# A four-layer graph network on one core: layer 0's preparation cut into pieces beside the second edge sort, and three of TensorE's turns in layer 3 placed behind a group's second pair of slots

## The reference

```
edge_index = jnp.stack([src, dst])
h = jnp.maximum(_layernorm(x, axis=-1), 0.0)
x = x + _L0_gnn_ref(h, edge_index, W, att_src, att_dst, bias)
...            # layers 1, 2 and 3 in the same way
```

```
h = (x @ W.T).reshape(N, H, C)                    # 4 heads of 64 channels
a_s = jnp.einsum('nhc,hc->nh', h, att_src)
a_d = jnp.einsum('nhc,hc->nh', h, att_dst)
e = jax.nn.leaky_relu(a_s[src] + a_d[dst], 0.2)
m = jax.ops.segment_max(e, dst, num_segments=N)
p = jnp.exp(e - m[dst])
alpha = p / (segment_sum(p, dst)[dst] + 1e-16)
out = segment_sum(alpha[:, :, None] * h[src], dst)
return elu(out + bias) + x
```

## Time and profile before

| | |
|---|---|
| median of 3 runs | 4839.82 us (4831.98 to 4845.45) |
| the profiled execution | 4839.27 us |
| its span | 4837.5 us |
| mean granted TensorE clock | 0.702 |
| busy: PE, DVE, ACT, POOL | 3143.0, 3130.4, 2247.6, 2855.6 us |

### The profile page before, as it was taken

The page is one execution under the profiler, slowest core; times in us unless marked ns, Lnnn a source line. Parts: engine busy times, 40 slices in busy tenths (PEclk is TensorE's granted clock), DMA queues, the critical chain, the costliest instruction groups (busy, mean ns, idle before and its releaser), DMA issues. The chain is left out here.

```text
span 4837.5 us, 75613 instructions
## 1 busy us (share of the span) xinstructions
PE 3143.0 (65%) x14588; PEld 2278.2 (47%) x14668; DVE 3130.4 (65%) x10392; ACT 2247.6 (46%) x8908; POOL 2855.6 (59%) x2739
## 2 busy tenths in 40 slices
PE   1588875777614666654777774466652677778776
PEld 0366664665512444443554453244431456566565
DVE  5887775666544555564777765476665477777776
ACT  0355554555422443344666664243334255555555
POOL 0377776777706777733777761777770265555532
PEclk9855556555556777676767767677776788888889
DMA  1000000000014444423454541444450476666641
GB/s 51 1 2 2 2 2 2 2 2 2 2 47 132 133 132 126 126 53 97 138 145 138 146 113 62 125 132 132 121 115 4 162 204 182 180 177 175 178 110 62
DMA packets 235835, 449.09 MB, mean 93 GB/s; under 512 B 80264, under 2 KB 132390, under 8 KB 235110
## 3 DMA queue, kind: packets, MB, share of 16 engines
q0 software_dynamic: 130816, 317.16, 25.1%
q1 hardware_dynamic: 104752, 128.89, 8.2%
HBM read 416.04 MB, written 29.80 MB: 92 GB/s over the span
## 5 line engine op out<-in xcount | busy, mean ns | idle before, releaser
L1239 POOL DMA_INDIRECT rows.4<-feats,by_dst_other.1 x464 | 506.2, 1091 | 537.8 <-issue 321.2
L1239 POOL DMA_INDIRECT rows.2<-feats,by_dst_other.1 x464 | 495.4, 1068 | 281.3 <-POOLq L976 140.2
L1239 POOL DMA_INDIRECT rows.1<-feats,by_dst_other.1 x464 | 493.4, 1063 | 280.7 <-POOLq L976 139.6
L1239 POOL DMA_INDIRECT rows.3<-feats,by_src_other.1 x448 | 476.4, 1063 | 256.9 <-issue 129.2
L658 POOL DMA_INDIRECT by_dst_records<-r_rec.1,r_idx.1 x448 | 443.8, 991 | 160.4 <-issue 127.7
L658 POOL DMA_INDIRECT by_src_records<-r_rec.2,r_idx.2 x416 | 413.9, 995 | 144.1 <-issue 113.4
L1455 ACT ACTIVATE rows.4<-rows.4,xres.1 128x65 f32<-128x65 f32 x1856 | 447.9, 335 | 0.9
L1455 ACT ACTIVATE rows.2<-rows.2,e_prob.2 128x33 f32<-128x33 f32 x1856 | 397.9, 314 | 0.0
L1370 PE MATMUL m_p.4<-rows.4,xres.1 128*128 128x264 f32 x1044 | 337.3, 451 | 30.9 <-issue 18.5
L1351 PE MATMUL m_p.3<-rows.3,m_oh.3 128*128 128x260 f32 x896 | 314.5, 505 | 13.9 <-DVE rows.3 L1604 13.0
L1622 DVE TENSOR_TENSOR acc.4<-acc.4,m_p.4 128x528 f32 x261 | 183.5, 703 | 198.3 <-PE m_p.4 L1387 155.9
(11 more groups left out here) (763 smaller groups left out, 8262.7 us busy)
## 6 DMA issues: line engine op xcount, KB each, us to landing
e_line.1<-by_dst_own_row SPq DMA_DIRECT2D x29, 512.0 KB, 5.0
e_line.2<-by_dst_own_row SPq DMA_DIRECT2D x29, 512.0 KB, 4.4
e_line.4<-by_dst_own_row SPq DMA_DIRECT2D x58, 256.0 KB, 5.2
e_line.3<-by_src_own_row SPq DMA_DIRECT2D x28, 512.0 KB, 5.0
xres.1<-by_dst_masks SPq DMA_DIRECT2D x232, 48.0 KB
e_mask.2<-by_dst_masks SPq DMA_DIRECT2D x29, 320.0 KB
rows.1<-feats,by_dst_other.1 POOLq DMA_INDIRECT x464, 2.8
rows.2<-feats,by_dst_other.1 POOLq DMA_INDIRECT x464, 3.9
```

The lines of the kernel that those rows point to most:

```text
L1239: pool.indirect_dma_start(out=rows[:, s % RING, :], out_offset=None, in_=feats, in_offset=bass.IndirectOffsetOnAxis(ap=g.other[:, s:s + 1] ...
```

## The change

Two things change.

**Layer 0's preparation.** A class `Front` holds what `read_sorted` does for `by_dst` and what layer 0's two blocks of norm and product do, as pieces with a batch number n. The second `place_edges` (that of `by_src`) gets it: ACT, PE and DVE run all 104 batches written out, without a loop, and do piece n behind batch n. POOL keeps its loop. The reading of the sorted edges has the batches 0 to 21, the norm 22 to 33, and tile t of the product begins at batch 34 + 8t // 3, with its steps in the five batches from there on; the last one ends in batch 102. The two PSUM banks of the finished histograms serve all of it (`by_lo` for turned tiles, `by_other` for products), one bank each where the product had two. SP issues the loads, the stores of masks and joins and the stores of the 25 tiles in the same block. Behind the second sort stands `read_sorted` for `by_src` alone, and then layer 0's `stream_edges`.

**Layer 3's turns.** With `LATE`, the turns 0, 1 and 2 of layer 3 stand behind the group's second pair and its closing; `turn_back` stays between the pairs. The order of DVE, ACT, POOL and SP in layer 3 is the same as before.

```diff
+        front = Front(nc, sig, sb, first, C, T, [hist[g].sums for g in graphs])
+        place_edges(nc, sig, sb, ps, second, C, B, T, None, front)
+    read_sorted(nc, sig, sb, ps, second, C)
-        place_edges(nc, sig, sb, ps, second, C, B, T, None)
-    for g in graphs:
-        read_sorted(nc, sig, sb, ps, g, C)
...
+class Front:
+    def tile_at(self, t):
+        return 34 + t * 8 // 3
...
+    def scalar(self, act, n):
...
+        if n in range(22, 27):
+            i = n - 22
+            act.wait_ge(S["steps"].sem, self.nmean_at(i))
...
+            for j in range(5):
+                t = 5 * i + j
+                ins = act.activation(self.sq[:, j, :], xres[:, t, :], ACT.Square, bias=self.nmean[:, t:t + 1], accum_out=self.ss[:, t:t + 1])
...
+            if n == self.tile_at(t) + 2:
+                act.wait_ge(S["tile_turned"].sem, S["tile_turned"].at(t + 1))
...
+                act.activation(self.hT[:, par, :, :], self.by_lo[:, 0:2 * P].rearrange("p (k q) -> p k q", k=2), ACT.Copy).then_inc(S["copied"].sem, 1)
+            if n == self.tile_at(t):
...
+                act.activation(self.hst[:, par, :], xres[:, t, :], ACT.Relu, bias=self.shift[:, t:t + 1],
+                               scale=self.rstd[:, t:t + 1]).then_inc(S["staged"].sem, 1)
+    def tensor(self, pe, n):
...
+            if n == self.tile_at(t) + 3:
+                pe.wait_ge(S["copied"].sem, S["copied"].at(t + 1))
+                if t >= 1:
+                    pe.wait_ge(S["evacuated"].sem, S["evacuated"].at(t))
...
+                for k in range(2):
+                    ins = pe.matmul(self.by_other[:, 0:CH + 8], self.hT[:, par, k, :], self.wall[:, k, :], start=k == 0, stop=k == 1)
+                ins.then_inc(S["product"].sem, 1)
+            if n == self.tile_at(t) + 1:
+                pe.wait_ge(S["staged"].sem, S["staged"].at(t + 1))
...
+                    ins = pe.transpose(self.by_lo[:, k * P:(k + 1) * P], self.hst[:, par, k * P:(k + 1) * P], ident[:, :])
+                ins.then_inc(S["tile_turned"].sem, 1)
+    def vector(self, dve, n):
...
+            if n == self.tile_at(t) + 4:
+                dve.wait_ge(S["product"].sem, S["product"].at(t + 1))
...
+                dve.tensor_copy(C["own0"][:, t, :], self.by_other[:, CH + 4:CH + 8]).then_inc(S["evacuated"].sem, 1)
...
@@ place_edges
+            if front is not None and eng_front is not None:
+                for i in range(trips):
+                    for quarter in range(Q):
+                        for part in parts:
+                            part(i * Q + quarter, quarter, i)
+                        eng_front(eng, i * Q + quarter)
+                return
...
@@ gat_layer_in
+    if n > 0:
+        norm_and_product(nc, sig, sb, ps, A, K, n, convs, heads0, wide, row0, own, feats)
...
@@ stream_edges
+    LATE = (NC == 2, NC == 2, NC == 2, False)
...
                         for k, turn in enumerate(turns):
-                            if AT[k] == i - 1:
+                            if AT[k] == i - 1 and not LATE[k]:
                                 turn(c + 1)
                     if PAIRS:
                         opening(s0 + 4 * i + 2, group + 1)
...
+                    if c + 1 < NCH:
+                        for k, turn in enumerate(turns):
+                            if AT[k] == i - 1 and LATE[k]:
+                                turn(c + 1)
```

More of the change, by code:

```diff
@@ L514, in place_edges, with _, turns @@
         trips = g.cols // (Q * B)
-        def turns(eng, parts, beside):
+        if front is not None:
+            front.place(c2)
+            @block.sync
+            def _(sp):
+                front.sync(sp)
+        def turns(eng, parts, beside, eng_front=None):
             def batches(i, ps):
@@ L566, in _ @@
             table(0, 0, 0)
-            turns(act, [ahead(diagonals, 2), ahead(table, 1), records], [])
+            turns(act, [ahead(diagonals, 2), ahead(table, 1), records], [], front and front.scalar)
         @block.tensor
@@ L607, in _ @@
             count(0, 0, 0)
-            turns(pe, [ahead(spread, 1), look, ahead(count, 1)], [lambda n, quarter, i: other.count(pe, n, quarter % 2)])
+            turns(pe, [ahead(spread, 1), look, ahead(count, 1)], [lambda n, quarter, i: other.count(pe, n, quarter % 2)], front and front.tensor)
         @block.vector
@@ L644, in _ @@
             onehots(0, 0, 0)
-            turns(dve, [before_in_column, ahead(onehots, 1), place], [lambda n, quarter, i: other.onehots(dve, n, quarter % 2)])
+            turns(dve, [before_in_column, ahead(onehots, 1), place], [lambda n, quarter, i: other.onehots(dve, n, quarter % 2)], front and front.vector)
         @block.gpsimd
@@ L669, in place_edges @@
         gate.base += Q * trips
+        if front is not None:
+            front.close()
 def read_sorted(nc, sig, sb, ps, g, C):
@@ L807, in gat_layer_in, with norm_and_product @@
     ROW = FROM + HS
-    own = sb("own_scores", [P, T, HS], F32, lc)
-    feats = nc.dram_tensor(f"feats{n}", [NT, ROW], F32, kind="Internal").ap()
+    own = K["own0"] if n == 0 else sb("own_scores", [P, T, HS], F32, lc)
+    feats = K["feats0"] if n == 0 else nc.dram_tensor(f"feats{n}", [NT, ROW], F32, kind="Internal").ap()
+    if n > 0:
+        norm_and_product(nc, sig, sb, ps, A, K, n, convs, heads0, wide, row0, own, feats)
+    with ExitStack() as c:
+        acc = sb("acc", [P, T, NC * max(wide) + (HS if n == 1 else 0)], F32, c)
+        stream_edges(nc, sig, sb, ps, K, n, g, convs, heads0, row0, own, feats, acc)
+        if n == 3:
+            finish_last(nc, sig, sb, ps, A, K, convs, acc, out)
+        elif n == 1:
+            finish_global(nc, sig, sb, ps, K, convs, acc)
+        else:
+            finish_layer(nc, sig, sb, ps, A, K, n, convs, acc)
+def norm_and_product(nc, sig, sb, ps, A, K, n, convs, heads0, wide, row0, own, feats):
+    N, T, NT, LAST = K["N"], K["T"], K["NT"], K["LAST"]
+    xres, ident = K["xres"], K["ident"]
+    NC = len(convs)
+    FEAT = NC * CH
+    HS = sum(c[1] for c in convs)
+    WALL = FEAT + 2 * HS
+    FROM = sum(wide)
+    ROW = FROM + HS
     steps, roots = sig("norm_steps"), sig("norm_roots")
@@ L1082, in gat_layer_in @@
             he.base += T + 2
-            hx.base += T if n in (0, 3) else 0
+            hx.base += T if n == 3 else 0
             for j in range(2):
                 st[j].base += 16 * (T // 2 + (1 - j) * (T % 2))
-    with ExitStack() as c:
-        acc = sb("acc", [P, T, NC * max(wide) + (HS if n == 1 else 0)], F32, c)
-        stream_edges(nc, sig, sb, ps, K, n, g, convs, heads0, row0, own, feats, acc)
-        if n == 3:
-            finish_last(nc, sig, sb, ps, A, K, convs, acc, out)
-        elif n == 1:
-            finish_global(nc, sig, sb, ps, K, convs, acc)
-        else:
-            finish_layer(nc, sig, sb, ps, A, K, n, convs, acc)
 def stream_edges(nc, sig, sb, ps, K, n, g, convs, heads0, row0, own, feats, acc):
```

244 lines of the change are left out of this document (234 added, 10 removed).

## The result

| | before | after |
|---|---|---|
| median of the runs made side by side | 4839.82 us (4831.98 to 4845.45) | 4664.69 us (4663.58 to 4666.39) |
| span of the profiled execution | 4837.5 us | 4663.4 us |
| mean granted clock | 0.702 | 0.723 |

The ratio is 0.964, with a 95% interval of 0.9623 to 0.9656. The prediction said 4665. One of its two large terms came out by the mechanism it named. The other came near its size by a way it had not priced: half of it or more is matmuls that run faster at a higher granted clock, which the prediction had put down as a rival.

What follows compares the result with a forecast made beforehand. It took POOL to bound the second sort and a PE-DVE round trip to pace layer 3. From 4839.3 us, less 102.5 for the preparation, plus 3 for the sort, less 75 for layer 3, it forecast 4665 us, range 4600 to 4725.

Steps and rivals of the forecast that it cites:

- The preparation's 102.5 us left the path: Between second sort and layer 0's stream: reading by_dst (42.3 us) and norm and product (60.2) leave the path.
- The 26.1 us of `by_src` stay: Reading block before layer 0's stream: its 26.1 us go with the graph's 112 partitions, not its place in the program.
- The sort loses 3 us: Second sort: taking up the preparation's work costs 3 us, between nothing and 53, as POOL stays the bound.
- TensorE is the tight one there, with 0.12 us a batch: Second sort: the product adds 0.95 us a batch into 1.07 us free on PE, leaving 0.12.
- Rival C: Second sort becomes bound by PE or locked-out scatters, say 30 us more: 4695 us, chance 0.08.
- the lock: Second sort: VectorE in a two-port mode locks GpSimd out of a shared port pair, costing up to 53 us.
- Layer 3 gives 75 us, as 1.0, 1.2 and 0.85 us a long chunk: Layer 3: moving turn_scores, turn_ends and turn_carry saves those three amounts, 3.0 us a long chunk and 1.8 a short one.
- Each of the three places gives its own gain: Layer 3: the gains at the three moved turns add up, 1.0, 1.2 and 0.85 us in a long chunk.
- Long chunks become 27.8: Layer 3: chunks of 30.8 us fall to about 27.8 us, and those of 26.8 to 25.
- Rival A: Layer 3's clock rises as PE idles less; twenty long chunks turn short for 56 us more: 4609 us, chance 0.14.
- rival B: Layer 3: DVE's chain ends each group, so removed waits come back; gain only 25 us: 4715 us, chance 0.12.

Runs made afterwards that it cites:

- front_only: The changed kernel with none of layer 3's turns moved, so only layer 0's preparation is changed: 4742.03 us, ratio 0.9809 to the kernel before.
- swapped: The kernel before with its two reading blocks in the other order, by_src first and by_dst second: 4843.96 us, ratio 1.0002.
- sort_pe3: The changed kernel with each tile's product done three times in the second sort: 4666.97 us, ratio 0.9641 to the kernel before.
- sort_dve2: The changed kernel with one more VectorE copy of 1024 float32 columns in each of the second sort's batches 34 to 103: 4681.25 us.
- turn0: The changed kernel with only turn_scores moved behind its group's second pair, turn_ends and turn_carry where they were before: 4659.59 us, ratio 0.9628.
- turns12: The changed kernel with only turn_ends and turn_carry moved behind their groups' second pairs, turn_scores where it was before: 4669.21 us, ratio 0.965.
- late_only: The kernel before with only the three turns of layer 3 moved, layer 0's preparation unchanged: 4770.19 us, ratio 0.9865.

## Why the prediction came out right

The forecast added up to 174.5 us (102.5 less 3, and 75); the span fell by 174.1. That it came this close is partly luck: layer 3 gave 5 us less than forecast, and the sort, which lost less, and layers 0 to 2, with 2.3 us that the change does not explain, made up for it. Term by term:

- *The preparation's 102.5 us left the path.* Right by its mechanism: 102.8 us between the last scatter and layer 0's first gather, 102 in `front_only`.
- *The 26.1 us of `by_src` stay, because they go with the graph.* Right: 25.9 us in after, and `swapped` shows it. The rule of the Trainium skill that the prediction used (DMA: Bandwidth & Descriptors, section "Why a DMA increments its semaphore by 16 and not by 1") agrees again: 9 tenths for 112 partitions in either place.
- *The sort loses 3 us.* Too much: the scatters' row is the same to 0.2 us, and the last one starts 0.9 us later, of which 1.1 had come before the first (795.92 for 794.81).
- *TensorE is the tight one there, with 0.12 us a batch.* Wrong, though the sum did not need it. I had priced the product at the low level for the whole of it. The clock rose to 0.69 instead, and in `sort_pe3` three times the product still fitted. Rival C rested on that price. Its other half, the lock, is real, but not for this change's instructions: scatters keep their 995 ns beside its evacuations from PSUM and its additions. Beside copies within SBUF, as `sort_dve2` has them, they don't.
- *Layer 3 gives 75 us, as 1.0, 1.2 and 0.85 us a long chunk.* The size was nearly right (69.9), the step was wrong, and so the size was luck. "Each of the three places gives its own gain" failed in `turn0` and `turns12`, where a part gave all. "Long chunks become 27.8" failed because there are none at that clock. Compared at one mean clock, chunks are 0.4 us shorter at 0.94 (27.7 to 27.3, on two chunks of before) and 1.1 to 1.4 at 1.00, not 1.8. How much of the 2.63 us is the clock's is an estimate: 1.3 by PE's busy time, some 2.2 by the step from chunks at 0.83 to chunks at 0.94. The rest is less idle time. The sum also took three long chunks for each short one from two chunks that it had looked at; there were 19 long, four at the full clock and three between, with nearly the same mean.
- *Rival A, the clock rises.* Its mechanism is in the runs (0.84 to 0.93 in layer 3), its 4609 us is not. I had put its 56 us on top of the 75, where it took the place of a good part of them. The chance of 0.14 had been for both together. And its "against", that the wait of 2 us only moves, was no argument: the wait moved, 2.3 us of it, and the clock did not fall there.
- *DVE's chain was the danger (rival B).* Half of it happened. The 2.0 us that PE had waited before `turn_scores` came back as 2.3 ahead of group 1's first pair, while the 1.1 before `turn_ends` went for good. PE's idle time still fell by 1.3 us a chunk. DVE's own work did not bound it: it is busy 21.9 us of each chunk, 27.3 or 25.0 us long.

Open: why orders with such different waits all end at a mean of 27.3 us a chunk. All of them have one fall or two of the clock in nearly every chunk; that the chunks and the clock's falls hold each other at this length is a rival that no run isolates. And which stretch of work brings on a fall was moved by the idle matmuls but not found.

## What to carry to other kernels

Before pricing a wait of TensorE, sort the repetitions of its loop by their granted clock and compare only those alike: here 19 chunks of 26 were nearly 4 us longer than the four at the full clock, with the same idle time, and no wait in the list said so. Price each of several moves alone on the chip before you add them up. And where "issue" stands beside TensorE in a run of tiny matmuls, try dealing them out behind longer matmuls: that was worth 47 us here, two thirds of what the turns gave, for two changed lines.

## What the runs showed of the hardware

- More work at no time, twice: 364 matmuls more in a stretch raised the granted clock from 0.50 to 0.79 and TensorE's busy time by 17 us of 264; seven idle matmuls a chunk made a kernel 0.4% faster.
- A VectorE copy of 128 x 1024 float32 within SBUF beside GpSimd's scatters made most of the scatters that it overlapped longer, by up to 0.55 us, 16 us in all for 70 copies; some copies took up to 0.96 us instead of 0.69.
- Runs of before lie from 4826 to 4850 us, with chunks of 26.8 to 31.1; those of after from 4663.6 to 4666.4, with chunks nearly alike. That the one makes the other is not shown: `late_only`, with chunks of 26.3 to 28.0, has runs within 1.7 us.
